# A fused two-layer graph kernel: other order and other engines in its first nine steps, type gathers spread

## The chip, the cores and the metric

The kernel runs on one core of one Trainium2 chip. The metric is the device time of one execution in microseconds (us). The engines are PE (TensorE), DVE (VectorE), ACT (ScalarE), POOL (GpSimd) and SP (SyncE, which here only issues DMAs). PE's clock is granted at one of two levels, 1.2 and 2.4 GHz; 1.00 in a row is the higher one over the whole stretch.

## The reference

50,000 nodes with 256 features and 12,500 edges; two layers, each followed by a layernorm over the features:

```python
qkv = x @ W_qkv.T + b_qkv
att = einsum('mhd,mhd->mh', Q[dst], K[src]) / sqrt(32)
a   = segment_softmax(att, dst)
x   = layernorm(x + segment_sum(a * V[src], dst) @ W_ff.T + b_ff)

cut  = where(edge_weight < 5, 0.5 * (cos(edge_weight * pi / 5) + 1), 0)
msgs = embed_table[node_type][src] * ((edge_attr @ W_dist + b_dist) * cut)
x    = layernorm(concat([x, segment_sum(msgs, dst)]) @ W_comb + b_comb)
```

Receivers `dst` come sorted; the kernel checks that, and sorts only where they don't.

## The kernel before, in words

All semaphores and the order of the work are written out by hand, one program for each engine; each engine goes through its own program in order. There are three stretches.

**Node steps** (`for g in range(G)`, G = 98): every step takes 512 rows of `x` through both layernorms as if no edge ended there. POOL adds `b_ff` (`z_add`, L704, tile `zin`, two buffers), DVE takes statistics (`stats`, L1392; `moments`, L1401), PE transposes the rows (L824) and ACT copies the result to `zT` (`zT_copy`, L1081), PE multiplies by the mixing weights `w_mix` in two halves (`z_product`, L845), DVE normalises (`y`, L1420, tile `yn`), ACT sums the squares (`squares`, L1096) and takes the root (`std2`, L1105), DVE inverts it (`rstd2`, L1430), and the last scaling (`final`, tile `on`) is shared: ACT does the first `split(g)` of the four row groups (L1113), and the rest is done by DVE (L1438) where the step is not "relaxed", by POOL (L714) where it is. "Relaxed" steps also have ACT's copy between its two halves of squares, and the inverse root one step later. Before, only steps from `AFTER` = 58 on are relaxed, with `split` 3 before them and 1 in them. SP loads four steps ahead and stores three steps behind.

**Edge work inside the node steps**: steps 9 to 57 (`LEAD` = 9) each carry one of 49 blocks of 256 edges. POOL gathers rows of `x` at both ends two blocks ahead (`gathers`: L723 `xd`, L726 `xs`) and the nodes' types (`type_gather`, L717, two of 98 columns a step). PE transposes the gathered rows (`columns`, L868, L873) and makes q, k and v in three passes of a high and a low part (L880 to L906; in these steps `z_product` too, L838 to L840). Steps 58 to 97 carry the softmax over edges instead (`softmax_step(g - AFTER)` on DVE). Steps 0 to 8 carry what the edge work needs: edge indices and cutoffs (`edge_floats`, `edge_cutoffs` with a sine on ACT, `edge_indices`), the weights' transposes and their two parts (`weight_copies`, `weight_low`), and the bias rows (`bias_parts`, L1482 to L1487).

**Last stretch**: once the softmax is done, the 49 blocks go through both layers again, and their rows are scattered over the output.

Ahead of the steps stand the constants, the centring of the weights (DVE, L1276 to L1296) and the order check: DVE compares neighbouring receivers (`pairs_gt`, L1290), PE adds up (L1011), DVE writes the flag (`unsorted`, L1299), and POOL and DVE read it and branch (L673). POOL's first sum stands behind that branch.

## Time and profile before

| | |
|---|---|
| median of three runs | 1139.29 us (1139.03 to 1140.47) |
| the profiled execution | 1139.81 us, span 1138.1 us |
| busy, share of the span | PE 93%, DVE 82%, POOL 71%, ACT 70% |
| steps 0 to 8 | from the first sum at 17.6 us to PE's first product of step 9 at 82.3 us |
| steps 9 to 57 | to about 556 us |
| steps 58 to 97, with the softmax | to about 749 us |
| last stretch | to the end |

In rows of the timeline the columns are start, duration, engine, line, operation, tiles and shapes, count, and in brackets the idle time of the engine before it with what ended that. In rows of the chain of waits they are start, duration, engine, tile and line. In rows of grouped instructions there follow the count, busy time in us and mean ns of one, then idle time of the engine before them and what ended it. In a table of stretches they are the stretch, its length, the busy time of PE, PE's weight loads, DVE, ACT and POOL (with counts), PE's granted clock, the DMA engines' busy share and GB/s.

### The profile page before, as it was taken

The page shows a single profiled execution, that of the slowest core. Times are in us where ns is not written, and L with a number is a line of the kernel's source. Part 1 is how long each engine was busy: PE and PEld are TensorE (multiplying, and loading weights), DVE is VectorE, ACT ScalarE, POOL GpSimd, SP SyncE. Part 2 cuts the span into 40 slices and gives each one's busy share as a digit, 9 for nine tenths or more (in the row PEclk, how much of TensorE's full clock was granted, in tenths as well). Part 3 has the DMA queues.
Part 4 walks back from the last instruction along what each step waited for, and adds up shares of the span by engine and source line. Part 5 has one row for each costly group of instructions (what it writes and reads, how often), then busy time and mean ns, then how long its engine had stood idle before and what let it go on. Part 6 is the DMA issues. An engine that isn't in the chain of part 4 may idle for free.

```text
span 1138.1 us, 25638 instructions
## 1 busy us (share of the span) xinstructions
PE 1062.5 (93%) x7302; PEld 985.0 (87%) x7302; DVE 928.7 (82%) x2662; ACT 794.4 (70%) x2432; POOL 806.9 (71%) x648
## 2 busy tenths in 40 slices
PE   4859999999999999999998799989999999999992
PEld 3759999999999999999877687879998888888882
DVE  4977888888877888777898989768888888888882
ACT  2957777777777777777776778865666666666663
POOL 4367888888888888888796768834666666666663
PEclk9979999999999999999999999989999999999997
DMA  4856666666766566666455557765666666666640
GB/s 150 281 210 216 221 229 218 225 226 217 221 220 221 200 223 223 222 212 211 183 202 189 181 208 238 268 203 165 171 179 182 183 185 184 188 190 190 192 130 33
DMA packets 121387, 227.26 MB, mean 200 GB/s; under 512 B 33587, under 2 KB 61486, under 8 KB 121184
## 3 DMA queue, kind: packets, MB, share of 16 engines
q1 hardware_dynamic: 104000, 189.54, 50.5%
q0 software_dynamic: 17248, 36.08, 10.6%
q8 instruction: 60, 0.98, 0.4%
q14 instruction: 79, 0.65, 0.2%
HBM read 137.84 MB, written 93.59 MB: 203 GB/s over the span
## 4 chain that ended last, share of the span: by engine, by line
PE 47%; DVE 24%; issue 11%; POOL 8%; ACT 6%; DMA 2%; DVEq 1%; ACTq 0%; SPq 0%; POOLq 0%
PE ps L845 9%; PE ps L824 5%; DVE num L1602 5%; PE ps L838 3%; PE ps L882 3%; PE ps L883 3%; PE ps L884 3%; PE ps L839 3%; PE ps L840 3%; DVE zeT L1613 3%; POOL zin L704 3%; DVE agg L1626 3%; DVE est L1639 3%; DVE msg L1622 2%; ACT t L1178 2%
## 5 line engine op out<-in xcount | busy, mean ns | idle before, releaser
L704 POOL TENSOR_TENSOR zin<-xin,bff_row 128x1024 f32<-128x1024 f32 x98 | 235.6, 2406 | 15.8 <-DVE stat L1392 10.2
L1420 DVE SCALAR_TENSOR_TENSOR yn<-ps,r,bc 128x256 f32<-128x256 f32 x391 | 169.2, 474 | 67.2 <-PE ps L840 44.3
L845 PE MATMUL ps<-w_mix,zT 128*128 128x256 f32 x780 | 189.7, 394 | 12.2 <-ACT zT L1081 9.7
L845 PEld LDWEIGHTS ps<-w_mix,zT 128*128 128x128 f32 x780 | 147.3, 196 | 36.5 <-ACT zT L1081 12.6
L1096 ACT ACTIVATE junk<-yn 128x256 f32<-128x256 f32 x391 | 157.7, 415 | 12.9 <-DVE yn L1420 12.9
L1392 DVE BATCH_NORM_STATS2 stat<-zin 128x6 f32<-128x256 f32 x391 | 135.7, 409 | 13.5 <-POOL zin L704 13.5
L733 POOL TENSOR_TENSOR ev<-abc,v 128x512 f32<-128x512 f32 x49 | 62.1, 1268 | 116.0 <-DVE zeT L1613 113.8
L723 POOL DMA_INDIRECT xd<-in_x_dram,idx x98 | 94.5, 964 | 37.4 <-issue 21.8
L745 POOL DMA_INDIRECT out_dram<-oe,idx x98 | 101.7, 1037 | 25.5 <-issue 20.7
L838 PE MATMUL ps<-mix_hi,z_hi 128*128 128x256 f32 x392 | 114.8, 293 | 2.7 <-DVE z_lo L1457 2.7
L726 POOL DMA_INDIRECT xs<-in_x_dram,idx x98 | 93.7, 956 | 29.9 <-issue 28.3
L717 POOL DMA_INDIRECT ty<-in_node_type_dram,src_i x98 | 93.7, 956 | 29.6 <-issue 29.3
L839 PE MATMUL ps<-mix_lo,z_hi 128*128 128x256 f32 x392 | 110.5, 282 | 0.0
L840 PE MATMUL ps<-mix_hi,z_lo 128*128 128x256 f32 x392 | 110.2, 281 | 0.0
L824 PE MATMUL ps<-ident,xin 128*128 128x128 f32 (+1 forms) x782 | 104.3, 278 | 0.0
L965 PE MATMUL ps<-wc,agg 128*128 128x256 f32 x392 | 98.3, 379 | 0.0
L824 PEld LDWEIGHTS ps<-ident,xin 128*128 128x128 f32 (+1 forms) x782 | 93.1, 144 | 6.0 <-issue 1.0
L1113 ACT ACTIVATE on<-yn,r 128x256 f32<-128x256 f32 x212 | 94.3, 500 | 0.2 <-DVE r L1430 0.2
L947 PE MATMUL ps<-num,wff 128*128 128x256 f32 x392 | 94.4, 384 | 0.0
L714 POOL TENSOR_TENSOR on<-yn,r 128x768 f32<-128x768 f32 (+1 forms) x41 | 59.9, 1460 | 47.1 <-DVE r L1430 47.1
L1145 ACT ACTIVATE vT<-ps,bqkv 128x256 f32<-128x256 f32 x98 | 41.2, 472 | 70.6 <-PE ps L906 70.6
L1196 ACT ACTIVATE oe<-ye,er 128x256 f32<-128x256 f32 x98 | 44.5, 501 | 61.5 <-DVE er L1662 61.5
(210 smaller groups left out, 3390.8 us busy)
## 6 DMA issues: line engine op xcount, KB each, us to landing
xin<-in_x_dram SPq DMA_DIRECT2D x97, 512.0 KB, 4.3
out_dram<-on SPq DMA_DIRECT2D x97, 512.0 KB
xd_o<-xdT SPq DMA_DIRECT2D x49, 256.0 KB
v_o<-vT SPq DMA_DIRECT2D x49, 256.0 KB
v<-v_o SPq DMA_DIRECT2D x49, 256.0 KB
xd<-xd_o SPq DMA_DIRECT2D x49, 256.0 KB, 4.1
abc<-a_o SPq DMA_DIRECT2D x196, 64.0 KB
sbc<-same_o SPq DMA_DIRECT2D x49, 128.0 KB, 3.8
```

The costliest lines, as they stand in the source:

```text
L704: pool.tensor_tensor(z, xx, bb, ALU.add).then_inc(n_z, 1)
L723: pool.indirect_dma_start(xd[:, par, t, :], None, x, bass.IndirectOffsetOnAxis(idx[:, n, 2 + t:3 + t], 0)).then_inc(e_g[par], 16)
L745: pool.indirect_dma_start(out, bass.IndirectOffsetOnAxis(idx[:, n, 4 + t:5 + t], 0), oe[:, par, t, :], None, bounds_check=N - 1, oob_is_er ...
L824: last = pe.transpose(ps[:, c, j * P:j * P + np_], xin[0:np_, q, j * D + c * P:j * D + (c + 1) * P], ident[0:np_, 0:np_])
L838: mm(to, hi, mix_hi[:, k, :], start=k == 0, stop=False)
L839: mm(to, hi, mix_lo[:, k, :], start=False, stop=False)
L840: last = mm(to, lo, mix_hi[:, k, :], start=False, stop=k == DC - 1)
L845: last = mm(ps[0:np_, half(g, j), (j % 2) * D:(j % 2 + 1) * D], zT[:, g % 2, k, j * P:j * P + np_], w_mix[:, k, :], start=k == 0, stop=k = ...
L965: last = mm(to[:, t, :], cols_of[:, k, t * P:(t + 1) * P], weights[:, k, :], start=k == 0 and not bias, stop=k == DC - 1)
L1096: last = act.activation(junk[0:np_, j, :], yn[0:np_, q, j * D:(j + 1) * D], ACT.Square, scale=float(D ** -0.5), accum_out=ss[0:np_, q, j:j ...
L1392: last = dve.bn_stats(stat[0:np_, g % SLOTS, j, :], zin[0:np_, g % 2, j * D:(j + 1) * D])
L1420: last = dve.scalar_tensor_tensor(out=yn[0:np_, q, j * D:(j + 1) * D], in0=ps[0:np_, half(g, j), (j % 2) * D:(j % 2 + 1) * D], scalar=r1[0 ...
```

## The change

Steps 0 to 8 become relaxed: POOL takes two of the four row groups of `final`, ACT two, and DVE none. In steps 57 to 81 ACT takes two instead of one and POOL two instead of three. POOL's first two sums go ahead of the branch; on DVE the mixing weights go ahead of the comparison of receivers, and on PE the transposes of step 0 ahead of the weights' column mean. ACT takes one root of a constant before anything else. The eight loads of edge rows go into SP's first two steps, and floats, cutoffs, sine and indices one or two steps earlier. Three copies of the bias rows go from DVE to ACT. The first four gathers go two to a step into steps 5 to 8, each behind the sum and the final of its step, and `gathers` is written as `receivers` and `senders`. The type gathers go from two in each of steps 9 to 57 to one and two by turns there, and one in each of steps 58 to 82.

```diff
 def relaxed(g):
-        return g >= AFTER
+        return g < LEAD or g >= AFTER
 def split(g):
-        return 1 if relaxed(g + 1) else 3
+        return 3 if not relaxed(g + 1) else 2 if g < AFTER + B // 2 else 1
...
 @block.sync
-            if g < 4:
-                edge_rows(g, (src_o, dst_o, dst_o[1:E], weight_o)[g])
+            if g < 2:
+                for k in range(2 * g, 2 * g + 2):
+                    edge_rows(k, (src_o, dst_o, dst_o[1:E], weight_o)[k])
...
 @block.gpsimd
+        pool.iota(lane_i[:], [[0, 1]], base=0, channel_multiplier=1).then_inc(s_lane, 1)
+        pool.wait_ge(s_w1, 16 * 4)
+        pool.wait_ge(s_wchain, 7)
+        for g in range(2):
+            z_add(g)
         pool.wait_ge(o_flag, 1)
         with pool.If(pool.value_load(unsorted[0:1, 0:1], min_val=0, max_val=E) > 1):
...
-        pool.iota(lane_i[:], [[0, 1]], base=0, channel_multiplier=1).then_inc(s_lane, 1)
-        pool.wait_ge(s_w1, 16 * 4)
-        for g in range(3):
-            z_add(g)
+        z_add(2)
         for g in range(G):
-            if g == LEAD - 3:
-                pool.wait_ge(s_idx, 1)
-                gathers(0)
-            if g == LEAD - 2:
-                gathers(1)
             if inside(g + 3):
                 z_add(g + 3)
             b = g - LEAD
             if within(b) and within(b + 2):
-                gathers(b + 2)
+                receivers(b + 2)
+                senders(b + 2)
             if within(b):
-                type_gather(2 * b)
-                type_gather(2 * b + 1)
-            if relaxed(g - 1):
+                type_gather(b)
+                if b % 2 == 1:
+                    type_gather(B + b // 2)
+            if B + B // 2 + g - AFTER in range(B + B // 2, T):
+                type_gather(B + B // 2 + g - AFTER)
+            if inside(g - 2) and relaxed(g - 1):
                 final(g - 2)
+            if g == LEAD - 4:
+                pool.wait_ge(s_idx, 1)
+            if g == LEAD - 4 or g == LEAD - 2:
+                receivers((g + 4 - LEAD) // 2)
+            if g == LEAD - 3 or g == LEAD - 1:
+                senders((g + 3 - LEAD) // 2)
...
 @block.tensor
-        pe.wait_ge(s_wchain, 7)
-        for k in range(DC):
-            last = mm(ps[:, 3, 0:D], ones_mean[:], wc[:, k, :], start=k == 0, stop=k == DC - 1)
-        last.then_inc(s_cm, 1)
...
         x_transposes(0)
+        pe.wait_ge(s_const, 2)
+        pe.wait_ge(s_wchain, 7)
+        for k in range(DC):
+            last = mm(ps[:, 3, 0:D], ones_mean[:], wc[:, k, :], start=k == 0, stop=k == DC - 1)
+        last.then_inc(s_cm, 1)
...
-            if g == 5:
+            if g == 3:
                 edge_columns()
...
 @block.scalar
+        def bias_copies():
+            act.wait_ge(s_w, 16 * 7)
+            act.activation(b_raw[:, 2, :], bc[:], ACT.Copy).then_inc(s_blow, 1)
+            act.wait_ge(s_blow, 1)
+            act.activation(b_rows[0:1], b_raw[0:1], ACT.Copy).then_inc(s_brow, 1)
+            act.activation(b_hi[HD:HD + 1], b_raw[HD:HD + 1], ACT.Copy).then_inc(s_blow, 1)
...
+        act.wait_ge(s_hs, 3)
+        act.activation(first_root[:], one_col[:], ACT.Sqrt, bias=eps_col[:])
...
+            if g == 4:
+                act.wait_ge(s_echain, 7)
+                act.activation(ct[:, 3, :], ct[:, 2, :], ACT.Sin, bias=half_pi[:], scale=-float(np.pi) / CUTOFF).then_inc(s_sin, 1)
...
             if g == 5:
-                act.wait_ge(s_echain, 7)
-                act.activation(ct[:, 3, :], ct[:, 2, :], ACT.Sin, bias=half_pi[:], scale=-float(np.pi) / CUTOFF).then_inc(s_sin, 1)
+                bias_copies()
...
 @block.vector
+        dve.wait_ge(s_cm, 1)
+        for c in range(DC):
+            dve.tensor_tensor(w_mix[:, c, :], wc[:, c, :], ps[:, 3, 0:D], ALU.subtract).then_inc(s_wready, 1)
         dve.wait_ge(o_rows, 16 * 4)
         dve.tensor_tensor(pairs_gt[:], pairs_i[:, 0, :], pairs_i[:, 1, :], ALU.is_gt).then_inc(o_gt, 1)
...
         def bias_parts():
-            dve.wait_ge(s_w, 16 * 7)
-            dve.tensor_copy(b_raw[:, 2, :], bc[:]).then_inc(s_blow, 1)
-            dve.wait_ge(s_blow, 1)
-            dve.tensor_copy(b_rows[0:1], b_raw[0:1]).then_inc(s_brow, 1)
-            dve.tensor_copy(b_hi[HD:HD + 1], b_raw[HD:HD + 1]).then_inc(s_blow, 1)
             dve.wait_ge(s_blow, 2)
             dve.tensor_tensor(b_rows[HD:HD + 1], b_raw[HD:HD + 1], b_hi[HD:HD + 1], ALU.subtract).then_inc(s_brow, 1)
...
             if inside(g - 1) and not relaxed(g):
+                if relaxed(g - 1):
+                    dve.wait_ge(n_od, g - 1)
                 final(g - 1)
-            if g == 4:
+            if g == 2:
                 edge_floats()
+            if g == 3:
+                edge_cutoffs()
             if g == 5:
-                edge_cutoffs()
-            if g == 6:
                 edge_indices()
```

Where a table of turns moves work, the engines' programs show it. The first place is POOL from its sums to the first step with edge work; before, and then with the change (`zin` sums, `xd` and `xs` gathers of rows, `ty` gathers of types, `on` finals).

```order
L704 TENSOR_TENSOR zin<-xin,bff_row 128x1024 x9
L723 DMA xd<-in_x_dram,idx 128x256 x2
L726 DMA xs<-in_x_dram,idx 128x256 x2
L704 TENSOR_TENSOR zin<-xin,bff_row 128x1024
L723 DMA xd<-in_x_dram,idx 128x256 x2
L726 DMA xs<-in_x_dram,idx 128x256 x2
L704 TENSOR_TENSOR zin<-xin,bff_row 128x1024 x3
L723 DMA xd<-in_x_dram,idx 128x256 x2
L726 DMA xs<-in_x_dram,idx 128x256 x2
L717 DMA ty<-in_node_type_dram,src_i 128x1 x2
```

```order
L730 DMA xd<-in_x_dram,idx 128x256 x2
L682 TENSOR_TENSOR zin<-xin,bff_row 128x1024
L721 TENSOR_TENSOR on<-yn,r 128x512
L736 DMA xs<-in_x_dram,idx 128x256 x2
L682 TENSOR_TENSOR zin<-xin,bff_row 128x1024
L721 TENSOR_TENSOR on<-yn,r 128x512
L730 DMA xd<-in_x_dram,idx 128x256 x2
L682 TENSOR_TENSOR zin<-xin,bff_row 128x1024
L721 TENSOR_TENSOR on<-yn,r 128x512
L736 DMA xs<-in_x_dram,idx 128x256 x2
L682 TENSOR_TENSOR zin<-xin,bff_row 128x1024
L730 DMA xd<-in_x_dram,idx 128x256 x2
```

Eight gathers that stood four and four between sums now stand two and two, with a sum and a final between each pair.

The second place is POOL in two successive edge steps; before, and then with the change.

```order
L704 TENSOR_TENSOR zin<-xin,bff_row 128x1024
L723 DMA xd<-in_x_dram,idx 128x256 x2
L726 DMA xs<-in_x_dram,idx 128x256 x2
L717 DMA ty<-in_node_type_dram,src_i 128x1 x2
L704 TENSOR_TENSOR zin<-xin,bff_row 128x1024
L723 DMA xd<-in_x_dram,idx 128x256 x2
L726 DMA xs<-in_x_dram,idx 128x256 x2
L717 DMA ty<-in_node_type_dram,src_i 128x1 x2
```

```order
L682 TENSOR_TENSOR zin<-xin,bff_row 128x1024
L730 DMA xd<-in_x_dram,idx 128x256 x2
L736 DMA xs<-in_x_dram,idx 128x256 x2
L724 DMA ty<-in_node_type_dram,src_i 128x1 x2
L682 TENSOR_TENSOR zin<-xin,bff_row 128x1024
L730 DMA xd<-in_x_dram,idx 128x256 x2
L736 DMA xs<-in_x_dram,idx 128x256 x2
L724 DMA ty<-in_node_type_dram,src_i 128x1
```

One type gather in two steps is gone from here.

The third place is POOL at the beginning of the softmax steps; before, and then with the change (`neg_a` and `neg_b` are masks of the softmax).

```order
L714 TENSOR_TENSOR on<-yn,r 128x768
L770 TENSOR_SCALAR neg_a<-same_c 112x896
L704 TENSOR_TENSOR zin<-xin,bff_row 128x1024
L714 TENSOR_TENSOR on<-yn,r 128x768
L773 TENSOR_SCALAR neg_b<-next_c 112x896
L704 TENSOR_TENSOR zin<-xin,bff_row 128x1024
L714 TENSOR_TENSOR on<-yn,r 128x768
```

```order
L721 TENSOR_TENSOR on<-yn,r 128x512
L782 TENSOR_SCALAR neg_a<-same_c 112x896
L682 TENSOR_TENSOR zin<-xin,bff_row 128x1024
L724 DMA ty<-in_node_type_dram,src_i 128x1
L721 TENSOR_TENSOR on<-yn,r 128x512
L785 TENSOR_SCALAR neg_b<-next_c 112x896
L682 TENSOR_TENSOR zin<-xin,bff_row 128x1024
L724 DMA ty<-in_node_type_dram,src_i 128x1
L721 TENSOR_TENSOR on<-yn,r 128x512
```

A gather of types has come in behind each sum, and the finals are two row groups wide in place of three.

## Rows read from the trace of the kernel before

**Rows 1.** Table of stretches (columns above).

```profile
25.90:82.30 56.40, 41.69 (x221) 35.48 (x220) 48.22 (x164) 40.97 (x130) 30.00 (x19) 0.88 0.66 236
76.00:88.00 12.00, 7.68 (x42) 7.34 (x43) 11.83 (x38) 9.02 (x27) 6.85 (x6) 0.58 0.33 107
100.00:112.00 12.00, 12.00 (x104) 11.94 (x103) 9.31 (x27) 8.34 (x24) 10.28 (x9) 1.00 0.53 184
570.00:670.00 100.00, 88.16 (x453) 75.10 (x452) 90.37 (x281) 70.60 (x235) 72.94 (x40) 0.93 0.54 191
```

**Rows 2.** Chain of waits, PE's first transposes of edge blocks 1, 2, 47 and 48.

```profile
92.66 0.44 PE ps L868 x4
102.10 0.44 PE ps L868 x4
...
535.40 0.44 PE ps L868 x4
545.24 0.44 PE ps L868 x4
```

**Rows 3.** Groups of POOL's instructions from 100 to 545 us.

```profile
L704 POOL TENSOR_TENSOR zin<-xin,bff_row 128x1024 f32<-128x1024 f32 x46 | 110.7, 2406 | 0.8
L717 POOL DMA_INDIRECT ty<-in_node_type_dram,src_i x91 | 86.8, 954 | 27.7 <-issue 27.4 <-DVE stat L1392 0.3
```

**Rows 4.** Timeline of the first 26 us.

```profile
11.32 0.35 DVE L1286 TENSOR_SCALAR bc<-bc,bc_mean 128x256 f32<-128x256 f32 x1
13.89 0.29 DVE L1290 TENSOR_TENSOR pairs_gt<-pairs_i 98x128 f32<-98x128 int32 x1 [2.22 <-DMA pairs_i<-in_dst_dram]
15.73 0.15 DVE L1299 CAST unsorted<-ps 1x1 int32<-1x1 f32 x1 [0.57 <-PE ps L1011]
17.58 14.11 POOL L704 TENSOR_TENSOR zin<-xin,bff_row 128x1024 f32<-128x1024 f32 x6
19.96 1.41 DVE L1392 BATCH_NORM_STATS2 stat<-zin 128x6 f32<-128x256 f32 x4 [4.08 <-POOL zin L704]
25.90 0.86 DVE L1420 SCALAR_TENSOR_TENSOR yn<-ps,r,bc 128x256 f32<-128x256 f32 x2
```

**Rows 5.** Instructions that touch `xin`, the second and third early loads.

```profile
L463 SPq DMA_DIRECT2D xin<-in_x_dram x2: 427/430/432, 10.7 to 11.2; - x2
...
DMA to landing us min/median/max: 5.3/5.7/6.1
```

**Rows 6.** Timeline, steps 5 to 9.

```profile
52.60 1.28 ACT L1088 ACT_TABLE_LOAD   x1
58.53 1.14 POOL L723 DMA_INDIRECT xd<-in_x_dram,idx  x1 [13.46 <-DVE lane L1385]
65.89 1.41 DVE L1392 BATCH_NORM_STATS2 stat<-zin 128x6 f32<-128x256 f32 x4 [4.56 <-POOL zin L704]
70.18 5.67 DVE L1484 CAST b_rows<-b_raw 1x768 fp32r<-1x768 f32 x1
70.78 4.65 POOL L704 TENSOR_TENSOR zin<-xin,bff_row 128x1024 f32<-128x1024 f32 x2
82.26 0.55 PE L838 MATMUL ps<-mix_hi,z_hi 128*128 128x256 f32 x1 [2.66 <-DVE z_lo L1457]
```

**Rows 7.** Groups of ACT's and DVE's instructions from 25.9 to 82.3 us.

```profile
L1113 ACT ACTIVATE on<-yn,r 128x256 f32<-128x256 f32 x21 | 9.1, 501 | 0.0
L1438 DVE TENSOR_SCALAR_CACHE_REDUCE on<-yn,r 128x256 f32<-128x256 f32 x8 | 3.8, 478 | 0.2
L1485 DVE CAST b_hi<-b_raw 1x768 fp32r<-1x768 f32 x1 | 0.6, 551 | 0.0
```

**Rows 8.** Timeline, one sum on POOL and one small softmax product on DVE.

```profile
590.89 2.35 POOL L704 TENSOR_TENSOR zin<-xin,bff_row 128x1024 f32<-128x1024 f32 x1
590.92 2.44 DVE L1550 TENSOR_TENSOR thr<-row 1x112 f32<-1x112 f32 x1
```

**Rows 9.** Groups of POOL's instructions from 556 to 700 us.

```profile
L714 POOL TENSOR_TENSOR on<-yn,r 128x768 f32<-128x768 f32 x26 | 38.2, 1468 | 35.6 <-DVE r L1430 35.6
```

More of the change, by code:

```diff
@@ L669, in move, with z_add @@
             pool.wait_ge(q_out, 64 * (t + 1))
+        def z_add(g):
+            q = g % SLOTS
+            np_, nj = size(g)
+            pool.wait_ge(n_x[q], 16 * (g // SLOTS + 1))
+            after(pool, n_st, g - 1)
+            z = zin[0:np_, g % 2, 0:nj * D].rearrange("p (j d) -> p j d", j=nj)
+            xx = xin[0:np_, q, 0:nj * D].rearrange("p (j d) -> p j d", j=nj)
+            bb = bff_row[0:np_, :].rearrange("p (a d) -> p a d", a=1).to_broadcast([np_, nj, D])
+            pool.tensor_tensor(z, xx, bb, ALU.add).then_inc(n_z, 1)
+        pool.iota(lane_i[:], [[0, 1]], base=0, channel_multiplier=1).then_inc(s_lane, 1)
[3 more added lines that the diff above has]
+            z_add(g)
         pool.wait_ge(o_flag, 1)
@@ L717, in type_gather, with receivers @@
             pool.indirect_dma_start(ty[:, t, :], None, ntype_rows, bass.IndirectOffsetOnAxis(src_i[:, t:t + 1], 0)).then_inc(n_ty, 16)
-        def gathers(n):
+        def receivers(n):
             par = n % 2
@@ L849, in edge_columns @@
         def edge_columns():
+            pe.wait_ge(o_flag, 1)
             pe.wait_ge(s_ef, 1)
@@ L1292, in _ @@
         dve.tensor_reduce(descents[:], pairs_gt[:], AX.X, ALU.add).then_inc(o_desc, 1)
-        dve.wait_ge(s_cm, 1)
-        for c in range(DC):
-            dve.tensor_tensor(w_mix[:, c, :], wc[:, c, :], ps[:, 3, 0:D], ALU.subtract).then_inc(s_wready, 1)
         dve.wait_ge(o_sum, 1)
-        dve.tensor_copy(unsorted[:], ps[0:1, 4, 0:1]).then_inc(o_flag, 1)
+        dve.tensor_copy(unsorted[:], ps[0:1, 7, 0:1]).then_inc(o_flag, 1)
         dve.wait_ge(o_flag, 1)
@@ L1671, in _ @@
                 y(g - 1, 1)
-            if relaxed(g - 1):
+            if inside(g - 2) and relaxed(g - 1):
                 rstd2(g - 2)
```

18 lines of the change are left out of this document (5 added, 13 removed).

## The prediction

> **What bounds the kernel now.** I read the table of stretches first, then the chain of waits for the pace, then the groups and timeline of the engines that the pace points to.
>
> In steps 0 to 8 nothing is full: between DVE's first `y` and PE's first product of step 9 (56.4 us) DVE is busy 48.2, PE 41.7 at a clock of 0.88, ACT 41.0, POOL 30.0 [rows 1]. The engines wait for each other by turns: DVE 4.56 us for a sum that stood behind four gathers, these behind the edge indices, and 5.67 us in one copy of 768 numbers on one partition, which on another partition took 0.55 [rows 6, 7]. That copy ends with POOL's two sums, which ran from 70.78 to 75.43.
>
> In steps 9 to 57 PE looks full (12.00 of 12) [rows 1]. But the pace changes: blocks 1 and 2 are 9.44 us apart, blocks 47 and 48 9.84 [rows 2]. What has that later pace is POOL: over 444 us its 46 sums waited 0.8 us in all [rows 3], so it never rests. From block 1 to 48 the chain took 452.6 us; 47 times 9.44 is 443.7. So 9 us of this stretch are POOL's.
>
> In the softmax steps DVE is the fullest (90.4 of 100; PE 88.2, ACT 70.6, POOL 72.9) [rows 1], and POOL's finals waited 35.6 us for DVE's inverse root [rows 9]. The last stretch isn't touched.
>
> **The change, part by part.** Durations are the profiled execution's; its own time is 1139.8 us (span 1138.1 and 1.7 around it), 0.5 over the median.
>
> *Start, -2.0 us (-3.3 to -0.8).* POOL's first sum waited for the branch, 17.58 us; now it waits for DVE's last centring, done at 11.67 [rows 4]. POOL needed 1.7 us from the flag (15.88) to its sum; I give DVE's branch the same, so its statistics can begin at 17.6, where they waited 4.08 us for the sum and began at 19.96. The third sum now waits for these statistics (19.0 and a sum of 2.35 makes 21.4, from 22.3 before, when it followed the second), and the third statistics begin at 21.4 in place of 24.6 (the end of the third sum before: 17.58 and three of 2.35). So `y` can be 3.2 to 3.3 us earlier. Against it: the comparison of receivers now comes behind two subtractions (0.86 as the pair of `y` [rows 4]), about 14.7 us, and beside it POOL starts its second sum as soon as its rows land. The third and fourth loads were issued at 10.7 and 11.2 and landed 5.3 and 6.1 us later, at 16.0 and 17.3 [rows 5]; one such spacing earlier is 14.7 for the second. Where the sum wins, the comparison waits for its end: a product of 112 numbers took 2.44 us while a sum of 2.35 us ran beside it [rows 8]. That takes 2.4 of the gain back. It is a toss-up; I take the middle. The Trainium skill ("SBUF — State Buffer", section "Who interferes with whom") has the rule that speaks against the new place of the sums: a DVE instruction with two SBUF inputs and a GpSimd instruction that reads SBUF exclude each other, whichever starts first, for the whole instruction. By that the gain is 0.8 or 3.2 and nothing between; rows 6 and 8 agree with it. ACT's early root takes a table load (1.28 [rows 6]) out of the start, but PE waits for the comparison's sum before its product then, so I give nothing for it.
>
> *Steps 0 to 8, -10.2 us (-15 to -5).* Take each engine's work in the 56.4 us [rows 1] and move it [rows 7]. DVE loses eight finals (3.8), the 5.67 and 0.55 of the bias copies and a third of about 0.3 (another 256-wide copy): 48.2 becomes 37.9. ACT gives up seven row groups (21 become 14) at 0.50, 3.5, and takes three copies: one 256 wide at 0.50, two 768 wide, between one such and three (0.5 to 1.5 each; I take 0.75): 41.0 becomes 39.5. POOL takes two groups of eight finals, two thirds of 1.47 each [rows 9]: 30.0 becomes 37.8. PE is 36.7 at full clock (41.7 times 0.88). So no engine is long any more and ACT is the longest. If it reached the share that DVE has now (48.2 of 56.4), the stretch would take 46.2 us: -10.2. With next to no waiting it would be about 41 (ACT 39.5 of it): -15. Were the side work still in series to half of what it gains, -5. The side work, spread one or two steps wider, is covered by the same engines' slack; the two table loads for the sine (1.28 each) can't be covered by ACT itself. The loads of edge rows are issued earlier on SP's queue, and only ahead of loads whose slots are still four steps away: nothing.
>
> *Block 0, -1.0 us (0 to -1.8).* From PE's first product of step 9 to block 1 it took 10.4 us (82.26 to 92.66 [rows 2, 6]) in a stretch with a clock of 0.58 [rows 1]; at full clock it is the pace of 9.44 less two transposes of 0.44, 8.6. PE idles less before it now; half.
>
> *A new wait at the end of step 9, +2.5 us (0 to 5).* DVE's first own final (of step 8) must wait for POOL's last (of step 7), which stands in POOL's step 9 behind a sum, four gathers and a type gather. A gather costs 0.954 and 27.7/91 of idle issue, 1.26 [rows 3]. From the edge indices on POOL has four sums (9.4), 13 gathers (16.4) and four finals (3.9): 29.7 us. DVE has three steps of 46.2/8.5 = 5.4 and one of 9.44 with its tail of about 1.5 behind it: 27.2. What queues behind it on DVE is the next `y`, the statistics and the low part that PE's q product waits for. Once; DVE has 2.7 us to spare in each 12 [rows 1].
>
> *Steps 9 to 57, -9.0 us (-9.4 to 0).* Half a type gather less in each step: POOL's 9.84 becomes 9.21, under PE's 9.44. The 9 us of above go.
>
> *Steps 57 to 82, +0.5 us (-2 to +5).* POOL gets a gather (1.26) and loses a row group (0.49) in 25 steps: 19 us, into 35.6 us of waiting [rows 9]. ACT gets 25 times 0.50, 12.5 us, where it is busy 70.6 of 100 [rows 1]. 26 finals in 144 us are 5.5 us a step; POOL then needs 2.4 + 1.0 + 1.3 = 4.7. Hidden, but for the masks' steps, where POOL had no rest. If gathers and DVE's copies held each other up too, each of some ten softmax operations might lose half a microsecond: +5; a shorter final ahead of the sum may free DVE's products earlier: -2.
>
> Sum: -2.0 - 10.2 - 1.0 + 2.5 - 9.0 + 0.5 = -19.2, 1120.6 on the profiled scale, 1120.0 as a median.
>
> **The rivals.**
> - *The edge stretch is PE's after all.* For: PE 12.00 of 12 [rows 1]. Against: POOL's sums that waited 0.8 us in 444 [rows 3]. Then 9 us stay: 1129.
> - *ACT takes DVE's place in steps 0 to 8.* For: it is the longest there after the change (39.5 us), with the sine, the bias copies and the weights in four steps running. Against: its row groups shrink from three to two. Only half of the 10.2 comes: 1125.
> - *POOL's sums hold DVE in the start and in the softmax steps alike.* For: rows 6 and 8. Against: there were as many sums before. 1.2 more at the start and 5: 1127.
> - *POOL falls behind in steps 57 to 82.* It decides once steps there are shorter than POOL's 4.7 us; then each of the 25 steps grows by the 0.77 added (19 us), and sums slide to where DVE's products start, ten of which wait half a sum (12 us): 1151. For: the masks' steps at the start; against: the 35.6 us [rows 9].
>
> **How the numbers follow.** A measurement of this kernel can tell about 0.2% (2.3 us) from no change. Forecast (1114 to 1126 by the bounds of its terms) 0.58; the first rival 0.12, the second 0.14, the third 0.08, POOL falling behind 0.05, and 0.03 for a first stretch without any waiting, under 1114. Only POOL falling behind ends at or over 1137: slower 0.04, same 0.02 with its lesser forms, faster 0.94. The range leaves out that rival and the extremes of the bounds: 1110 to 1130.
>
> **What would show it.** First `y` near 23.9 us; DVE's copy of 5.67 gone and three copies on ACT; PE's first product of step 9 near 70; one late q product in step 10; blocks 1 to 48 apart by 9.44 throughout (443.7 us) and POOL's sums waiting again; finals on POOL with less waiting in the softmax steps and their length unchanged at about 193 us. Wrong it is if the blocks keep 9.84 at the end, if step 9 still begins after 77, or if the softmax steps take over 198 us.

## The result and the profile after

The changed kernel took 1123.97 us (median; 1123.25 to 1127.21, 4 runs) beside 1139.41 of the kernel before on the same chip: a ratio of 0.9871, with a 95% interval of 0.9854 to 0.9887. Run again as the first experiment it took 1124.97 (1124.64 to 1126.77), ratio 0.9880 (0.9864 to 0.9895). It is faster, by 14 to 15 us where I had forecast 19.2; 1124 lies inside the range, 4 us above the forecast.

There are two profiles of it. The first was taken of an execution of 1127.2 us (span 1125.5), the second of one of 1124.6 (span 1123.0), which is near the median. I use the second where I don't say otherwise. Its page:

```profile
span 1123.0 us, 25645 instructions
## 1 busy us (share of the span) xinstructions
PE 1059.6 (94%) x7302; PEld 984.6 (88%) x7302; DVE 918.8 (82%) x2643; ACT 802.9 (71%) x2452; POOL 811.1 (72%) x656
```

To see where the time went I cut every span at six marks, the starts of instructions in the timelines: DVE's first `y`; PE's first product of step 9 (the first of its three passes, which waits for the low part `z_lo`); the first transposes of edge blocks 1 and 2; the transposes of tile 59 (first of step 58) and of tile 87 (step 86, behind the last softmax operation). The kernel before has them at 25.90, 82.26, 92.50, 101.94, 557.81 and 705.15 (the chain view of [rows 2] puts the same transposes 0.16 later), the changed one at 22.57, 69.91, 80.03, 92.19, 537.83 and 692.23.

| stretch, us | before | first profile | second | second less before | forecast |
|---|---|---|---|---|---|
| to the first `y` | 25.90 | 22.59 | 22.57 | -3.3 | -2.0 |
| to step 9's product | 56.36 | 48.35 | 47.34 | -9.0 | -10.2 |
| to block 1 | 10.24 | 9.00 | 10.12 | -0.1 | -1.0 |
| block 1 to 2 | 9.44 | 14.80 | 12.16 | +2.7 | +2.5 |
| block 2 to tile 59 (edge) | 455.87 | 445.58 | 445.64 | -10.2 | -9.0 |
| tile 59 to 87 (softmax) | 147.34 | 154.40 | 154.40 | +7.1 | +0.5 |
| to the end | 432.95 | 430.78 | 430.77 | -2.2 | 0 |
| sum | 1138.1 | 1125.5 | 1123.0 | -15.1 | -19.2 |

**Start.** The timeline of the second profile, which answers to [rows 4] (DVE's and POOL's rows):

```profile
11.31 0.35 DVE L1308 TENSOR_SCALAR bc<-bc,bc_mean 128x256 f32<-128x256 f32 x1
11.80 2.34 POOL L682 TENSOR_TENSOR zin<-xin,bff_row 128x1024 f32<-128x1024 f32 x1 [8.28 <-DVE bc L1308]
...
14.63 0.28 DVE L1316 TENSOR_TENSOR pairs_gt<-pairs_i 98x128 f32<-98x128 int32 x1
14.63 2.49 POOL L682 TENSOR_TENSOR zin<-xin,bff_row 128x1024 f32<-128x1024 f32 x1 [0.48 <-DMA xin<-in_x_dram]
...
17.29 1.40 DVE L1414 BATCH_NORM_STATS2 stat<-zin 128x6 f32<-128x256 f32 x4 [1.53 <-POOL zin L682]
...
22.57 0.86 DVE L1442 SCALAR_TENSOR_TENSOR yn<-ps,r,bc 128x256 f32<-128x256 f32 x2
```

The sum starts on DVE's last centring, as worked out. The toss-up fell the good way: comparison and second sum start in the same hundredth, the comparison takes 0.28, and it is the sum that is 0.12 longer.

**Steps 0 to 8.** First the stretch in the table of stretches ([rows 1]), then rows of the timeline: SP's one-row tail loads, who waits for loads, the bias copies on ACT, and PE's product.

```profile
22.57:69.91 47.34, 40.23 (x220) 34.61 (x220) 40.12 (x146) 41.58 (x128) 32.76 (x22) 0.96 0.82 286
```

```profile
19.64 3.94 SPq L491 DMA_DIRECT2D rows_i<-dst_o  x1
...
24.41 2.21 SPq L491 DMA_DIRECT2D rows_i<-dst_o  x1
...
26.96 3.28 SPq L491 DMA_DIRECT2D rows_f<-weight_o  x1
...
28.64 2.37 POOL L682 TENSOR_TENSOR zin<-xin,bff_row 128x1024 f32<-128x1024 f32 x1 [2.79 <-DMA xin<-in_x_dram]
...
34.18 0.36 DVE L1371 CAST rows_f<-rows_i 98x384 f32<-98x384 int32 x1 [3.75 <-DMA rows_f<-weight_o]
...
50.59 0.40 ACT L1137 ACTIVATE b_raw<-bc 128x256 f32<-128x256 f32 x1
51.02 0.84 ACT L1139 ACTIVATE b_rows<-b_raw 1x768 fp32r<-1x768 f32 x1
51.88 0.85 ACT L1140 ACTIVATE b_hi<-b_raw 1x768 fp32r<-1x768 f32 x1
...
69.91 0.36 PE L845 MATMUL ps<-mix_hi,z_hi 128*128 128x256 f32 x1 [2.77 <-DVE z_lo L1479]
```

The 5.67 us of [rows 6] are gone, ACT is the longest engine (41.6 of 47.3), and the stretch is 9.0 shorter. New is what SP does: three loads of one row (336, 332 and 336 bytes) held its queue for 9.4 us, and DVE and POOL stood for what came behind them.

**Block 0.** To block 1 it took 10.1 us in the second profile and 9.0 in the first. The difference is PE's clock in the 6 us behind step 9's first product; second profile, then first (PE's busy time first, the granted clock third from the end):

```profile
69.91:75.91 6.00, 6.00 (x38) 6.00 (x39) 5.70 (x19) 4.51 (x15) 5.34 (x5) 0.72 0.63 212
```

```profile
70.94:76.94 6.00, 5.78 (x47) 5.58 (x48) 5.69 (x19) 4.75 (x15) 5.35 (x5) 1.00 0.74 252
```

At 1.00 PE ran 47 matmuls there, at a mean of 0.72 only 38. In all the profiles below that leave these steps as they are, this stretch takes 9.0 or 10.1 us, nothing between; so 1.1 us there tells nothing of an edit.

**The end of step 9.** POOL's product of tile 7 and DVE's wait for it, second profile, then first:

```profile
81.56 1.05 POOL L721 TENSOR_TENSOR on<-yn,r 128x512 f32<-128x512 f32 x1
...
82.65 0.48 DVE L1460 TENSOR_SCALAR_CACHE_REDUCE on<-yn,r 128x256 f32<-128x256 f32 x1 [3.83 <-POOL on L721]
```

```profile
82.63 1.05 POOL L721 TENSOR_TENSOR on<-yn,r 128x512 f32<-128x512 f32 x1
...
83.71 0.48 DVE L1460 TENSOR_SCALAR_CACHE_REDUCE on<-yn,r 128x256 f32<-128x256 f32 x1 [5.00 <-POOL on L721]
```

And the stretch behind it in the table of stretches, PE's busy time first and the granted clock third from the end, second profile, then first:

```profile
86.00:92.00 6.00, 6.00 (x51) 6.00 (x52) 4.69 (x15) 3.23 (x8) 4.48 (x6) 1.00 0.48 163
```

```profile
87.00:92.00 5.00, 5.00 (x29) 5.00 (x30) 2.97 (x11) 2.25 (x5) 3.78 (x5) 0.66 0.55 183
```

The wait is the one forecast. Where block 0 had gone 1.1 us faster (first profile) DVE only stood 1.2 longer. There PE's clock then fell, to a mean of 0.66 of its 2.4 GHz (the lower level is 0.5 of it); in the second profile it stayed at full. So a wait of 3.8 us cost 2.7 of the path and one of 5.0 cost 5.4. Of the seven experiments below that edit something and keep this wait, four profiles show the long form (14.9 to 16.0 us from block 1 to 2, waits of 5.0 to 5.1 or the clock low), and the runs of one kernel scatter by about as much.

**Edge stretch.** Groups of POOL's instructions, after (110 to 520 us), and the receivers' gathers of the same stretch before:

```profile
L682 POOL TENSOR_TENSOR zin<-xin,bff_row 128x1024 f32<-128x1024 f32 x45 | 108.2, 2405 | 0.8
L730 POOL DMA_INDIRECT xd<-in_x_dram,idx x86 | 82.6, 960 | 29.0 <-PE ps L876 11.9 <-issue 11.1 <-DVE stat L1414 6.1
```

```profile
L723 POOL DMA_INDIRECT xd<-in_x_dram,idx x84 | 80.9, 963 | 19.7 <-issue 19.2 <-PE ps L868 0.5
```

Before, these gathers stood 0.5 us for PE beside 19.2 of issue time; now 18 us for PE and DVE beside 11.1. The pace is PE's: block 2 to tile 59 took 445.4 to 445.7 us in every kernel below that has the change's spread.

**Softmax stretch.** Here the time was lost. Rows of DVE's softmax operations and POOL's sums, before:

```profile
565.24 1.17 DVE L1529 TENSOR_TENSOR next_c<-dcf 112x896 f32<-112x896 f32 x1
565.55 3.09 POOL L704 TENSOR_TENSOR zin<-xin,bff_row 128x1024 f32<-128x1024 f32 x1
...
569.62 0.93 DVE L1531 TENSOR_SCALAR first_c<-dcf 112x896 f32<-112x896 f32 x1
...
584.09 2.10 DVE L1545 TENSOR_TENSOR_SCAN seg_c<-neg_b,run_c 112x896 f32<-112x896 f32 x1
584.41 3.95 POOL L704 TENSOR_TENSOR zin<-xin,bff_row 128x1024 f32<-128x1024 f32 x1
```

and after:

```profile
545.15 2.36 POOL L682 TENSOR_TENSOR zin<-xin,bff_row 128x1024 f32<-128x1024 f32 x1
545.26 3.20 DVE L1546 TENSOR_TENSOR next_c<-dcf 112x896 f32<-112x896 f32 x1
...
551.57 2.37 POOL L682 TENSOR_TENSOR zin<-xin,bff_row 128x1024 f32<-128x1024 f32 x1
551.66 2.75 DVE L1548 TENSOR_SCALAR first_c<-dcf 112x896 f32<-112x896 f32 x1
...
568.17 2.37 POOL L682 TENSOR_TENSOR zin<-xin,bff_row 128x1024 f32<-128x1024 f32 x1
568.29 4.13 DVE L1562 TENSOR_TENSOR_SCAN seg_c<-neg_b,run_c 112x896 f32<-112x896 f32 x1
```

Before, the sum came 0.3 us behind the operation and waited for it (3.09 and 3.95 in place of 2.36). Now it comes 0.1 us ahead, and the operation waits for the sum's end: 2.0, 1.8 and 2.0 us more. POOL is earlier because its last product takes two row groups (1.04 us) and no longer three (1.47). DVE has no idle time in these steps (27.97 us busy of the 28 from 544 to 572), so this is lost at once. Added over all 37 softmax operations of the timeline, from `same_c` to the last product into `a_c`, DVE took 48.5 us before and 53.5 after: 5.0 of the 7.1.

### The profile page after: what moved, and what is told of

Read it like the earlier page. It is cut to its first block, busy times and chain, and to the rows that moved or that the text cites. A ratio compares the mean times of both kernels' runs of the same rounds, so it can differ in the third digit from the quotient of the medians.

```text
span 1125.5 us, 25645 instructions
## 1 busy us (share of the span) xinstructions
PE 1058.2 (94%) x7302; PEld 983.2 (87%) x7302; DVE 918.4 (82%) x2643; ACT 802.3 (71%) x2452; POOL 811.4 (72%) x656
## 4 chain that ended last, share of the span: by engine, by line
PE 52%; DVE 26%; issue 10%; ACT 7%; SPq 2%; DVEq 1%; DMA 1%; POOL 0%; ACTq 0%; POOLq 0%
PE ps L852 7%; DVE num L1619 5%; PE ps L831 5%; PE ps L891 4%; PE ps L890 4%; PE ps L892 4%; PE ps L847 4%; PE ps L845 4%; PE ps L846 4%; DVE zeT L1630 3%; DVE est L1656 3%; DVE agg L1643 3%; PE ps L888 2%; ACT t L1196 2%; DVE msg L1639 2%
## 5 line engine op out<-in xcount | busy, mean ns | idle before, releaser
L682 POOL TENSOR_TENSOR zin<-xin,bff_row 128x1024 f32<-128x1024 f32 x98 | 233.1, 2379 | 39.3 <-DVE stat L1414 18.5
L852 PE MATMUL ps<-w_mix,zT 128*128 128x256 f32 x780 | 189.4, 394 | 10.1 <-ACT zT L1092 5.4
L724 POOL DMA_INDIRECT ty<-in_node_type_dram,src_i x98 | 103.2, 1053 | 25.7 <-issue 23.1
L1124 ACT ACTIVATE on<-yn,r 128x256 f32<-128x256 f32 (+1 forms) x229 | 101.0, 498 | 0.2 <-DVE r L1452 0.2
L1092 ACT ACTIVATE zT<-ps,bff_col 128x512 f32<-128x512 f32 x98 | 61.8, 678 | 37.8 <-PE ps L831 37.6
```

What stands on the lines that cost most here:

```text
L682: pool.tensor_tensor(z, xx, bb, ALU.add).then_inc(n_z, 1)
L724: pool.indirect_dma_start(ty[:, t, :], None, ntype_rows, bass.IndirectOffsetOnAxis(src_i[:, t:t + 1], 0)).then_inc(n_ty, 16)
L852: last = mm(ps[0:np_, half(g, j), (j % 2) * D:(j % 2 + 1) * D], zT[:, g % 2, k, j * P:j * P + np_], w_mix[:, k, :], start=k == 0, stop=k = ...
L1124: last = act.activation(on[0:np_, q, j * D:(j + 1) * D], yn[0:np_, q, j * D:(j + 1) * D], ACT.Copy, scale=r2[0:np_, q, j:j + 1])
```

## The experiments

All kernels start from the changed one unless said; "second profile" is its own. Marks are those of the table.

**after_again**: no edit.

> The changed kernel itself, once more, to have a profile near its median and a tighter ratio. Its first profile was taken of the slowest of four executions (1127.2 us; median 1124.0). If that profile is typical, the marks here stand within 1 us of it: columns of block 0, 1, 2 start at 67.1, 80.1, 94.9; block 48 at 529.3; the last final of the softmax stretch at 682.7. If the extra 3.2 us of that execution were a slip in one place, one of these marks comes 2 to 3 us earlier here, and I would look for it in steps 57 to 81, where the loss was larger than I had bounded. Ratio 0.986 to 0.988.

Measured 1124.97 us (ratio 0.9864 to 0.9895). The 2.5 us between the two profiles lie, in sum, between block 1 and 2, in that wait and the clock behind it (the 1.0 in steps 0 to 8 and the 1.1 the other way in block 0 cancel); the softmax stretch took 154.40 in both, to the hundredth. My guess of a slip there was wrong: the loss in it is no accident.

**no_spread**: two type gathers in each edge step, none behind.

```
-                type_gather(b)
-                if b % 2 == 1:
-                    type_gather(B + b // 2)
-            if B + B // 2 + g - AFTER in range(B + B // 2, T):
-                type_gather(B + B // 2 + g - AFTER)
+                type_gather(2 * b)
+                type_gather(2 * b + 1)
```

> The changed kernel, but with the type gathers as before: two in every edge step, none behind it. Theory 1 (POOL sets the edge stretch, and the 25 gathers moved behind it are a part of the loss in steps 57 to 81): blocks stand 9.63 us apart again instead of 9.43, block 48 starts 9 us later, and steps 57 to 81 take 133 to 134 us instead of 137, so the whole is 4 to 6 us longer than the changed kernel (ratio to the kernel before about 0.991). Theory 2 (the late gathers are the whole loss of steps 57 to 81): those steps take 130 us again, and the whole is only 2 us longer. Theory 3 (the edge stretch gained by the looser order or the start, not by the spread): blocks stay 9.43 apart, and the whole is 3 to 7 us shorter than the changed kernel.

Measured 1134.77 (1134.32 to 1135.71; ratio 0.9948 to 0.9975), 10 us longer. The edge stretch took 455.1 (+9.5), the softmax stretch 150.3 (-4.1), block 1 to 2 14.9 (+2.8; a second gather stands ahead of the product DVE waits for). Theory 1: the spread is worth 9.5 us in the edge steps and costs 4.1 behind them; the whole grew by more than the 4 to 6 I had expected, since block 1 to 2 and the last stretch (+1.7) came out longer too. But 2.9 of the 7.1 stay without the late gathers, and next_c, first_c and seg_c take 3.19, 2.73 and 4.13 as in the changed kernel: theory 2 falls.

**gathers_late**: the 25 late gathers six steps later, behind the masks (and the copy of the types, which waits for them, five steps later).

```
-            if B + B // 2 + g - AFTER in range(B + B // 2, T):
-                type_gather(B + B // 2 + g - AFTER)
+            if B + B // 2 + g - AFTER - 6 in range(B + B // 2, T):
+                type_gather(B + B // 2 + g - AFTER - 6)
...
```

> The changed kernel with the 25 late type gathers moved from steps 58 to 82 to steps 64 to 88, behind the four mask products that POOL does in steps 59, 60, 63 and 64 (and the copy of the types five steps later). Theory 1 (the loss of steps 57 to 81 is POOL overfull where masks and gathers meet in its first five steps): the 5 us lost there come back and at most 1 or 2 are lost behind, so the whole is 3 to 5 us shorter. Theory 2 (POOL is full in all steps of this stretch, so a gather costs its 1 us wherever it stands until step 82): 0 to 2 us shorter, from the six gathers that now lie behind step 82 alone. Theory 3 (the loss is not the gathers' but that of POOL's sums running beside VectorE's softmax operations): no change.

Measured 1126.61 (1123.82 to 1126.97; ratio 0.9867 to 0.9897): no difference that the intervals show. The softmax stretch is 1.5 shorter, and the long form of block 1's wait (15.6) hides it. Next_c 3.19, first_c 2.73, seg_c 4.13: the masks don't care for the gathers. Theory 2, inside the stretch.

**final7_first**: in step 9, POOL does tile 7's product ahead of the gathers.

```
             b = g - LEAD
+            if g == LEAD:
+                final(g - 2)
...
-            if inside(g - 2) and relaxed(g - 1):
+            if inside(g - 2) and relaxed(g - 1) and g != LEAD:
                 final(g - 2)
```

> The changed kernel, but in step 9 POOL does the last product of tile 7 right behind its sum, ahead of the four gathers of block 2 and the type gather. Theory 1 (the 5.4 us that block 1 lost on its way to block 2 are VectorE's wait for that product, which POOL's order of gathers sets): the wait of 5.0 us on VectorE falls to under 1, block 2 starts 4 to 5 us earlier, and the whole is 4 to 5 us shorter. Theory 2 (block 2's gathers, now later by 1 to 2 us, or TensorE's own first blocks take the wait's place): block 2 starts 0 to 2 us earlier, the whole 0 to 2 us shorter.

Measured 1121.67 (1120.94 to 1123.32; ratio 0.9835 to 0.9865), 3.3 under the second measurement of the changed kernel, though the two intervals touch. The marks say it plainly: block 1 to 2 in 9.42 us, the pace of [rows 2], and DVE's operation behind no wait (its timeline):

```profile
75.30 1.05 POOL L721 TENSOR_TENSOR on<-yn,r 128x512 f32<-128x512 f32 x1
...
78.68 0.47 DVE L1462 TENSOR_SCALAR_CACHE_REDUCE on<-yn,r 128x256 f32<-128x256 f32 x1
```

The whole wait was POOL's order: theory 1.

**split1**: in steps 57 to 81 POOL's product takes three row groups again.

```
-        return 3 if not relaxed(g + 1) else 2 if g < AFTER + B // 2 else 1
+        return 3 if not relaxed(g + 1) else 2 if g < AFTER - 1 else 1
```

> The changed kernel, but in steps 57 to 81 POOL's last product takes three quarters of a tile again and ScalarE one, as before the change: POOL gets 0.43 us more work in each of these 25 steps. Theory 1 (the loss at the start of the softmax stretch is a toss-up between POOL's sum and VectorE's mask operation: in the profile of the changed kernel the sum starts 0.1 us ahead of the mask operation and holds it for 2 us, before the change it started 0.3 us behind it and waited itself): with 0.43 us more ahead of it the sum starts behind the mask operation again, next_c takes 1.2 us instead of 3.2, first_c 0.9 instead of 2.75, and at least the first of these two 2 us comes back: the whole is 2 to 5 us shorter, by more work on POOL. Theory 2 (POOL has too much work in these steps): 25 times 0.43 us more, up to 10 us longer, at least 3. Theory 3 (neither; VectorE's own work sets these steps): no change.

Measured 1129.50 (1128.12 to 1131.04; ratio 0.9897 to 0.9924): 4.5 longer. Yet the mask came out as theory 1 has it, by 0.43 us of more work ahead of the sum, which now starts 0.31 behind the mask:

```profile
548.62 1.17 DVE L1546 TENSOR_TENSOR next_c<-dcf 112x896 f32<-112x896 f32 x1
...
548.93 3.08 POOL L682 TENSOR_TENSOR zin<-xin,bff_row 128x1024 f32<-128x1024 f32 x1
```

That settles what turned next_c. Seg_c came back too (2.49), first_c in part (2.16). Behind them other operations lost more: the pair of `cr` took 4.75 (0.55 before), run_c with ex_c 5.53 (3.59 before, 4.18 after); all 37 operations 55.2 us, the stretch 156.7, 2.3 longer. Most of what this profile lost beyond that lies between block 1 and 2 (16.0 us). Theory 2 holds for the time. Its cause, POOL overfull, is not shown: the pair of `cr` stood beside POOL's product and sum and ended just behind them, which looks like the same interference at another place.

```profile
587.63 4.75 DVE L1529 TENSOR_TENSOR cr<-lr,far 1x112 f32<-1x112 f32 x2
588.20 1.48 POOL L721 TENSOR_TENSOR on<-yn,r 128x768 f32<-128x768 f32 x1
589.62 2.34 POOL L682 TENSOR_TENSOR zin<-xin,bff_row 128x1024 f32<-128x1024 f32 x1
```

**sums_wait**: in steps 59 to 82 a sum waits for the step's first `y`.

```
             if inside(g + 3):
+                if AFTER < g < AFTER + 25:
+                    pool.wait_ge(n_yy, 2 * g)
                 z_add(g + 3)
```

> The changed kernel, but in steps 59 to 82 POOL's sum waits until VectorE has done the first y of the step, so that it runs beside the stat and y operations and not beside VectorE's softmax operation. Theory 1 (the sums that start just ahead of a softmax operation hold it): the four mask and scan operations that were stretched (3.20, 2.75, 1.95, 4.13 us) go back to about 1.2, 0.9, 1.6 and 2.1, and the stretch from step 57 to 82 gets 4 to 7 us shorter. Theory 2 (POOL has too much work): the waits make POOL later still, the whole is 2 to 8 us longer. A rival within theory 1: the type gather or the last product takes the sum's place beside the softmax operation and holds it instead (they read the same memory), and the gain is 0 to 3 us.

Measured 1120.74 (1118.02 to 1121.85; ratio 0.9819 to 0.9846): 4.2 shorter by a wait that was added. The sum now ends before the mask begins:

```profile
544.00 2.37 POOL L682 TENSOR_TENSOR zin<-xin,bff_row 128x1024 f32<-128x1024 f32 x1 [8.88 <-DVE yn L1444]
```

```profile
546.67 1.06 DVE L1548 TENSOR_TENSOR next_c<-dcf 112x896 f32<-112x896 f32 x1
```

First_c took 1.16, seg_c 2.30, all 37 operations 43.4 us, under the 48.5 of before; the stretch 149.0, 5.4 shorter. Theory 1. It does not become shorter than before's 147.3, I think because POOL with its gathers is now what some steps wait for: there its sums follow each other 4.55 us apart where PE's step is 4.33. combo_gathers, below, bears that out.

**rows_on_act**: ScalarE issues the edge rows' loads.

```
-            if g < 2:
-                for k in range(2 * g, 2 * g + 2):
-                    edge_rows(k, (src_o, dst_o, dst_o[1:E], weight_o)[k])
...
+        for k, a in enumerate((src_o, dst_o, dst_o[1:E], weight_o)):
...
+            act.dma_start(to[0:full, k, :], a[0:full * P].rearrange("(t p) -> t p", p=P)).then_inc(s_rows, 16)
```

> The changed kernel, but the eight loads of the edge rows are issued by ScalarE, behind its first deviation, instead of by SP between the loads of x. Theory 1 (the short tail loads that SP issues behind a backlog cost it 0.6, 3.9, 2.2 and 3.3 us, which delays the edge rows, VectorE's cast that waits 3.7 us for them, and the next loads of x, for which POOL waits 6.5 us): the loads of x leave SP 5 us earlier, the cast waits under 1 us, block 0 starts 2 to 4 us earlier and the whole is 2 to 4 us shorter. Theory 2 (the tails are slow wherever they are issued): ScalarE is held 8 to 10 us early in step 0 or 1 instead, and the whole is 0 to 5 us longer. Theory 3 (VectorE has so much to do in steps 0 to 8 that the wait only moves to another place before block 0): no change.

Measured 1131.90 (1131.20 to 1133.37; ratio 0.9922 to 0.9949): 6.9 longer, and more than the 5 that theory 2 allowed. Theory 2 in its mechanism: the tails hold ScalarE's queue as they held SP's, and its next deviation starts at 29.85, 9.0 us later than in the changed kernel:

```profile
23.52 3.50 ACTq L1218 DMA_DIRECT2D rows_i<-dst_o  x1
...
29.85 0.30 ACT L1089 ACTIVATE sd<-mv,eps_col 128x4 f32<-128x4 f32 x1 [10.37 <-issue]
```

**bias_on_dve**: the three bias copies back on DVE in step 7.

```
-            if g == 5:
-                bias_copies()
...
+            dve.tensor_copy(b_raw[:, 2, :], bc[:]).then_inc(s_blow, 1)
+            dve.wait_ge(s_blow, 1)
+            dve.tensor_copy(b_rows[0:1], b_raw[0:1]).then_inc(s_brow, 1)
+            dve.tensor_copy(b_hi[HD:HD + 1], b_raw[HD:HD + 1]).then_inc(s_blow, 1)
```

> The changed kernel with the three copies of the bias rows back on VectorE in step 7 (ScalarE's three in step 5 took 2.1 us together). Theory 1 (they cost VectorE 6.5 us before, the first of them 5.67 us because it stood beside a sum on POOL, and VectorE sets steps 0 to 8): block 0 or the wait behind it comes 2 to 6 us later, and the whole is 2 to 6 us longer. Theory 2 (5.67 us was the overlap with that sum, and the copy alone is short; there is room in step 7): 0 to 1 us longer.

Measured 1123.45 (1122.83 to 1123.99; ratio 0.9846 to 0.9876): no difference. DVE's timeline shows the first copy, which ended at 64.68, behind POOL's sum and product beside it (to 64.52), and the wait at the end of step 9:

```profile
62.77 1.91 DVE L1502 COPY b_raw<-bc 128x256 f32<-128x256 f32 x1
...
82.40 0.48 DVE L1458 TENSOR_SCALAR_CACHE_REDUCE on<-yn,r 128x256 f32<-128x256 f32 x1 [1.87 <-POOL on L721]
```

The copies took 3.2 us together (1.91, 0.55, 0.73). Step 9's product came 2.0 later, block 1 1.7 later, and block 2 at 91.93 beside 92.19: DVE only waited less for POOL. So moving them to ACT gains 2.0 us up to step 9, and the wait behind it takes them back; the 5.67 us of [rows 6] were an overlap that the other edits moved away anyway. Theory 2 for the whole; whether the copies matter once the wait is gone was not tried.

**check_first**: POOL's first two sums behind the order check again.

```
-        for g in range(2):
-            z_add(g)
         pool.wait_ge(o_flag, 1)
...
-        z_add(2)
+        for g in range(3):
+            z_add(g)
```

> The changed kernel, but POOL's first two sums stand behind the check of the receivers' order again, as before the change. Theory 1 (the start's gain is POOL's sums that no longer wait for the check, and it is carried to block 0): the first sum starts at about 16 us instead of 11.8, and block 0 starts 2 to 4 us later than the 66.1 to 67.8 us of the runs with the changed start; as the product of tile 7 on POOL then holds block 1, 1 to 4 us of it show in the whole. Theory 2 (VectorE's wait for the edge rows takes the start's gain back): block 0 starts at the same time within 1 us, the whole within 1 us.

Measured 1126.83 (1125.65 to 1127.41; ratio 0.9869 to 0.9899). First sum and first `y` (25.53):

```profile
17.21 9.28 POOL L682 TENSOR_TENSOR zin<-xin,bff_row 128x1024 f32<-128x1024 f32 x4 [13.69 <-issue]
```

`y` is 3.0 later, step 9's product and block 1 2.6, the median 1.9 (which the intervals alone would not show). Theory 1: the start's gain is these two sums', and most of it arrives.

**combo**: final7_first and sums_wait together.

> The changed kernel with both edits that shortened it when made alone: POOL's product of tile 7 ahead of block 2's gathers in step 9, and POOL's sums behind the first y in steps 59 to 82. If they act in different places (start of the edge stretch; softmax stretch), their gains add: 3.3 and 4.2 us off the changed kernel's 1125, so 1116 to 1118 us, ratio to the kernel before about 0.981. If block 2's start only moves a slip to a later place that the sums' waits also move, the two overlap and it is 1119 to 1121.

Measured 1115.74 (1113.06 to 1116.30; ratio 0.9772 to 0.9799). The gains add (9.2 under the changed kernel, where 3.3 and 4.2 make 7.5): block 1 to 2 in 9.44, softmax stretch 148.2. It beats the kernel before by 24 us and the changed one by 9, well apart from its interval.

**combo_floats**: combo, with the edge rows' cast, columns, cutoffs and sine a step later each.

```
-            if g == 2:
+            if g == 3:
                 edge_floats()
-            if g == 3:
+            if g == 4:
                 edge_cutoffs()
```

> The kernel with both edits, and the edge rows' cast, columns, cutoffs and the sine one step later each (VectorE in steps 3 and 4, TensorE in 4, ScalarE in 5), so that VectorE does not stand before the rows that SP's slow tail issues bring late. Theory 1 (the wait of 3.7 us on VectorE for the rows is lost time, since VectorE sets steps 0 to 8): block 0 starts 2 to 4 us earlier, and with block 2 no longer held by POOL's product, the whole is 2 to 4 us shorter than the kernel with both edits. Theory 2 (POOL's sums, which stand 6.5 us for loads of x that the same tails delay, set these steps as much): 0 to 1 us. Theory 3 (the indices come later, and POOL's first gathers with them): 0 to 3 us longer.

Measured 1114.41 (1112.69 to 1116.20; ratio 0.9766 to 0.9793). The time can't be told from combo's. DVE's wait for the rows is gone (3.92 in combo), but step 9's product comes at 69.99 beside 69.97. Block 1 and 2 come 1.1 earlier by PE's clock alone, as between the two profiles of the changed kernel; the 6 us behind step 9's product, combo, then this kernel:

```profile
69.97:75.97 6.00, 6.00 (x38) 6.00 (x39) 5.69 (x19) 4.52 (x15) 5.51 (x5) 0.72 0.66 212
```

```profile
69.99:75.99 6.00, 5.77 (x47) 5.56 (x48) 5.70 (x19) 4.75 (x15) 5.51 (x5) 1.00 0.82 264
```

So no cost of DVE's wait for the rows is shown: theory 2 is nearest.

**combo_gathers**: combo, with 1.75 type gathers in an edge step and 13 behind the masks.

```
                 if b % 2 == 1:
                     type_gather(B + b // 2)
-            if B + B // 2 + g - AFTER in range(B + B // 2, T):
-                type_gather(B + B // 2 + g - AFTER)
+                if b % 4 == 2:
+                    type_gather(B + B // 2 + b // 4)
+            if 85 + g - AFTER - 7 in range(85, T):
+                type_gather(85 + g - AFTER - 7)
```

> The kernel with both edits, and 12 of the 25 late type gathers moved into the edge steps (1.75 per step instead of 1.5), the other 13 in steps 65 to 77. A gather takes POOL about 1.26 us of an edge step with its gap; by that POOL needs 9.0 us of a step with 1.5 gathers and 9.3 with 1.75, and TensorE's step is 9.43. Theory 1 (POOL has that much room in the edge stretch, and is full behind it): blocks stay 9.43 apart, the softmax stretch gets 2 to 4 us shorter, and the whole by as much. Theory 2 (two steps with two gathers in a row bring POOL behind TensorE now and then): blocks 9.45 to 9.55 apart, up to 5 us given back, the whole the same or up to 3 us longer.

Measured 1113.86 (1111.50 to 1115.03; ratio 0.9763 to 0.9790), the lowest median, though its interval overlaps combo's. In its profile the softmax stretch took 142.2 us, 6 less than combo's and 5 less than before; the edge stretch 446.1, 0.5 more. The receivers' gathers from 110 to 520 us have issue time alone again, so POOL's room in the edge steps is nearly used up:

```profile
L730 POOL DMA_INDIRECT xd<-in_x_dram,idx x86 | 82.5, 960 | 20.2 <-issue 20.2
```

## Why the prediction was right in sign and 4 us too low

- *Start* (-2.0, bound -3.3): measured -3.3. The mechanism was right, the toss-up between comparison and sum fell to the comparison in every profile of the changed start (first `y` at 22.3 to 22.6), and I had taken the middle. check_first shows that 2.6 of it reaches block 1. That the size is the bound's is luck, since I had no reason to expect the comparison first. The prediction has [rows 6] and [rows 8] agree with the rule that it cites, for a DVE instruction with two SBUF inputs; the copy of 5.67 us in [rows 6] has one input, so only [rows 8] is such a case.
- *Steps 0 to 8* (-10.2): -9.0, and -8.0 in the first profile. That ACT becomes the longest engine came true, 41.6 busy of 47.3. One step was wrong in what it says of the queue: "the loads of edge rows are issued earlier on SP's queue ... nothing". Two pairs of them in a row took SP's queue 10.1 us in tails (0.63, 3.94, 2.21, 3.28), where four spread steps had taken 4.4 (0.62, 2.72, 0.64, 0.47). DVE stood 3.75 and POOL 6.0 us for loads behind them. combo_floats took DVE's wait away and step 9 came no earlier, so no price of it is shown; what POOL's waits cost was not tried. Moving the bias copies gained 2.0 us in this stretch, not the 6.5 that DVE had spent on them, and nothing in the whole (bias_on_dve).
- *Block 0* (-1.0): -0.1 in one profile and -1.2 in the other. The mechanism was the clock, as forecast: where it stayed at full the stretch took 9.0 us (I had 8.6 for that), where it fell to a mean of 0.72 behind step 9's product, 10.1. In the first profile the wait behind it took the gain back.
- *A new wait at the end of step 9* (+2.5, up to 5): +2.7 and +5.4, the latter over its bound. Right in place, mechanism and what queued behind it; final7_first takes it away. Missing was that PE's clock can fall behind the wait, as it did in the first profile (0.66).
- *Steps 9 to 57* (-9.0): -10.2, of which no_spread gives the spread 9.5.
- *Steps 57 to 82* (+0.5, bounds -2 to +5): +7.1, outside the bounds and the main error. I counted POOL's work (19 us into 35.6 us of waiting, [rows 9]) and called it hidden. The work was not the matter: POOL got 0.43 us shorter ahead of a sum, the sum passed from 0.3 us behind DVE's mask to 0.1 us ahead of it, and three operations lost 2 us each where I had given ten of them half a microsecond. The step that failed is "a shorter final ahead of the sum may free DVE's products earlier: -2": the shorter final is what brought the sum ahead of them. no_spread shows 2.9 of the 7.1 without any late gather, split1 turns next_c and seg_c back by more work on POOL, sums_wait takes 5.4 back by a wait. The other 4.1 go when the late gathers go. By the sign I had set (softmax steps over 198 us, from 193) this term was wrong: 7.1 more makes 200. [Rows 8] showed such a pair (2.44 beside a sum of 2.35), and I read it as a size, not as an order that a tenth of a microsecond turns. The Trainium skill ("SBUF — State Buffer", section "Who interferes with whom") has that, of a DVE instruction with two SBUF inputs and a GpSimd instruction that reads SBUF, whichever issues first holds the shared ports for the whole instruction and the other waits; the rows of next_c in the two kernels (1.17 beside 3.09, 3.20 beside 2.36) agree with it in both directions.
- *The last stretch* (0): -2.2 in code that the change doesn't touch. At the seam behind the last step PE idles 3.9 us in either kernel and its clock falls to 1.2 GHz; it came back while the first product of the numerators ran, which took 2.93 us where it had taken 3.62, and the second product came 1.1 us sooner behind it. Another 0.9 lies behind the last such product (29.4 us to the end, 30.3 before), and no run shows why. In other kernels below the stretch is 430.7 to 432.5. I count none of it as a gain of the change.

That the whole came within 4 us is in part luck: the 6.6 us that I missed in the softmax steps were made up in part by the toss-up at the start (1.3), the edge steps (1.2) and a last stretch that the change doesn't touch (2.2).

Of the rivals, the third had the mechanism of the main error: POOL's sums holding DVE, priced at 5 us in the softmax steps. DVE's 37 operations there took 5.0 more, 3.1 of it without any late gather (51.6 in no_spread); its other half, at the start, did not come. POOL falling behind pointed at the same stretch, at 31 us; the 4.1 that the late gathers cost are what can be put to it. ACT, which was to take DVE's place in steps 0 to 8, can have cost at most what that stretch fell short by, 1.2 to 2.2. The first rival fell with no_spread.

Still open: why the short tail loads issue so slowly (they did from two queues; leaving them out was not tried); 0.7 us of the edge stretch that the spread doesn't account for; what holds `cr` and run_c longer in split1, the order alone or POOL's fuller program; and when PE's clock falls behind the first product and the wait of step 9 (after a wait of 3.83 us it stayed, after 3.85 in check_first it fell and block 1 to 2 took 13.7).
